# The second group norm's statistics taken inside the attention phase, by GpSimd

## The chip, the cores and the metric

One core of a Trainium2 chip (trn2) runs the whole kernel. The metric is the device time of one execution in microseconds, the median of several. TensorE (PE), VectorE (DVE), ScalarE (ACT), GpSimd (POOL) and SyncE (SP, which here only issues DMAs) run side by side and are ordered by semaphores alone.

## The reference, cut to what matters

The input `x` has 256 x 256 positions with 128 channels, f32. Two layers follow each other, both with a group norm (32 groups of 4 channels, statistics over all positions) at their head:

```python
def _gn(v, G=32, eps=1e-5):
    g = v.reshape(B_, H_, W_, G, C_ // G)
    m = jnp.mean(g, axis=(1, 2, 4), keepdims=True)
    s = jnp.var(g, axis=(1, 2, 4), keepdims=True)
    return ((g - m) / jnp.sqrt(s + eps)).reshape(v.shape)

x = x + attention(_gn(x))          # layer 0: rows of 256, 4 heads of 32
x = x + state_space(_gn(x))        # layer 1: conv, four scans, norm, product
```

The change touches the second `_gn` only, and of it only the two numbers for each group, mean and variance of the result of layer 0 (called `x1` here).

## The kernel before

The kernel is a sequence of phases with a barrier of all engines between them (`end_block`, L59 to L63): weights, `group_stats` "g0" on `x`, `norm_phase`, `attention_phase`, `group_stats` "g1" on `x1`, `conv_phase`, `scans_phase` (over 80% of the time), `output_phase`. All statements of a phase are unrolled, each engine has a program of its own, and an instruction waits on semaphores that count (`S["yev"]` at r + 1 means that row r has been added).

**Attention** (L285 to L544) runs over the 256 rows of the picture, r = 0 to 255. Each row is 256 positions x 128 channels, kept as [128 partitions, 2, 128]. The order on each engine is written out by hand, three rows deep: TensorE projects row r + 3, makes the scores of r + 2, turns the exponentials of r and mixes the values; ScalarE takes exponentials and moves results out of PSUM; VectorE adds the bias to the scores (L495), takes the row's maximum (L525), moves one head (L508), takes the reciprocal of the denominators (L504), gates (L529, L534), and adds the output product in PSUM to the row of `x` in the buffer `a_xt` (L516, semaphore `yev`). GpSimd has one operation a row: it spreads the eight reciprocals over 256 elements (L542, semaphore `spread`), and TensorE turns that tile (L418, `across`). SyncE stores eight rows of `a_xt` at a time to `x1` in DRAM (L357, a chunk; `a_xt` and `a_zt` hold four chunks), and then loads the next `zn_t` rows (L345) and `x` rows (L350) into the chunk that came free.

**The statistics** (`group_stats`, L66 to L141) read the tensor back from DRAM in four loads of 8 MB (L91) into two buffers, with `bn_stats` for each load and group on VectorE (L98, 128 in all), join them with `bn_aggr` for each group (L102, 32), and then work out the scale and the shift over the partitions: a product with a matrix of 1/128 (L130), small VectorE operations, a second product (L133), a root on ScalarE (L138), and for "g1" two columns with scale and shift of each channel (L122, L125).

**conv_phase** begins with one row loaded from `x1` (L608), turned and projected on TensorE, while VectorE clears the large buffer `c_xi` (L663) before the row may be put there.

Of the kernel before, what the change touches and what calls it, by code (L numbers as in the profile page):

```python
# [10 lines left out]
ALU = mybir.AluOpType  # L11
# [3 lines left out]
P = 128  # L15
# [36 lines left out]
def signals(sems, names):  # L52

    names = names.split()
    assert len(names) <= len(sems) and len(set(names)) == len(names)
    return dict(zip(names, sems))


def end_block(nc, sems):  # L59

    first = sems[0].num
    nc.vector.sem_clear(range(first, first + len(sems)))
    nc.all_engine_barrier()  # L63


def group_stats(nc, sems, name, x, eps, const, scale_row, shift_row, columns=None):  # L66

    CHUNK = BANK // PER_GROUP
    per_part = TOKENS // P
    chunks = per_part // CHUNK  # L70
    with ExitStack() as stack:
        m = Memory(nc, stack)
        xt = m.sb(f"{name}_x", [P, 2, CHUNK, C])
        st = m.sb(f"{name}_st", [P, GROUPS, chunks, 6])
        mv = m.sb(f"{name}_mv", [P, GROUPS, 2])
        avg = m.sb(f"{name}_avg", [P, GROUPS, 2])
        dev = m.sb(f"{name}_dev", [P, GROUPS])
        var = m.sb(f"{name}_var", [P, GROUPS])
        std = m.sb(f"{name}_std", [P, GROUPS])
        pick = m.sb(f"{name}_pick", [P, 2, GROUPS])  # L80
        total = m.ps(f"{name}_total", [P, 2, BANK])
        src = x.rearrange("(p j k) c -> j p k c", p=P, k=CHUNK)
        S = signals(sems, "load0 load1 stats aggr mean dev spread var std chain")

        with nc.Block() as block:
            @block.sync
            def _(e):
                for j in range(chunks):
                    if j >= 2:
                        e.wait_ge(S["stats"], j - 1)  # L90
                    e.dma_start(xt[:, j % 2], src[j]).then_inc(S[f"load{j % 2}"], DMA)  # L91

            @block.vector
            def _(e):
                for j in range(chunks):
                    e.wait_ge(S[f"load{j % 2}"], DMA * (j // 2 + 1))
                    for g in range(GROUPS):
                        last = e.bn_stats(st[:, g, j, :], xt[:, j % 2, :, g * PER_GROUP:(g + 1) * PER_GROUP])  # L98
                    last.then_inc(S["stats"], 1)
                e.wait_ge(S["stats"], chunks)  # L100
                for g in range(GROUPS):
                    last = e.bn_aggr(mv[:, g, :], st[:, g])  # L102
                last.then_inc(S["aggr"], 1)
                e.wait_ge(S["mean"], 1)
                e.tensor_copy(avg[:, :, :].rearrange("p g s -> p (g s)"), total[:, 0, 0:2 * GROUPS]).then_inc(S["chain"], 1)
                e.wait_ge(S["chain"], 1)
                e.tensor_tensor(dev[:, :], mv[:, :, 0], avg[:, :, 0], ALU.subtract).then_inc(S["chain"], 1)
                e.wait_ge(S["chain"], 2)
                e.tensor_tensor(dev[:, :], dev[:, :], dev[:, :], ALU.mult).then_inc(S["dev"], 1)
                e.wait_ge(S["spread"], 1)  # L110
                e.tensor_tensor(var[:, :], avg[:, :, 1], total[:, 1, 0:GROUPS], ALU.add).then_inc(S["chain"], 1)
                e.wait_ge(S["chain"], 3)
                e.tensor_scalar(var[:, :], var[:, :], eps, None, ALU.add).then_inc(S["var"], 1)
                e.wait_ge(S["std"], 1)
                e.reciprocal(scale_row[:, :], std[:, :]).then_inc(S["chain"], 1)
                e.wait_ge(S["chain"], 4)
                e.scalar_tensor_tensor(out=shift_row[:, :], in0=avg[:, :, 0], scalar=-1.0, in1=scale_row[:, :],
                                       op0=ALU.mult, op1=ALU.mult).then_inc(S["chain"], 1)
                if columns:
                    e.wait_ge(S["chain"], 5)  # L120
                    for i, row in enumerate((scale_row, shift_row)):
                        e.tensor_tensor(pick[:, i, :], row[:, :], const["group_of"][:, :], ALU.mult).then_inc(S["chain"], 1)  # L122
                    e.wait_ge(S["chain"], 7)
                    for i, column in enumerate(columns):
                        e.tensor_reduce(column[:, 0:1], pick[:, i, :], AX_X, ALU.add)  # L125

            @block.tensor
            def _(e):
                e.wait_ge(S["aggr"], 1)
                e.matmul(total[:, 0, 0:2 * GROUPS], const["mean"][:, :], mv[:, :, :].rearrange("p g s -> p (g s)"),  # L130
                         start=True, stop=True).then_inc(S["mean"], 1)
                e.wait_ge(S["dev"], 1)
                e.matmul(total[:, 1, 0:GROUPS], const["mean"][:, :], dev[:, :], start=True, stop=True).then_inc(S["spread"], 1)  # L133

            @block.scalar
            def _(e):
                e.wait_ge(S["var"], 1)
                e.activation(std[:, :], var[:, :], ACT.Sqrt).then_inc(S["std"], 1)  # L138
        end_block(nc, sems)
# [142 lines left out]
        end_block(nc, sems)  # L282


def attention_phase(nc, sems, x, zn_t, bias_d, x1, wts, const):  # L285

    N = SIDE
    CHUNK = zn_t.shape[2] // SIDE
# [3 lines left out]
    with ExitStack() as stack:  # L292
# [12 lines left out]
        spread = m.sb("a_spread", [P, 2, JB, C])  # L305
        factor = m.sb("a_factor", [P, 2, SIDE])
        gt = m.sb("a_gt", [P, 2, SIDE])
        scores = m.ps("a_scores", [P, HEADS, BANK])
        proj = m.ps("a_proj", [P, BANK])
        turn = m.ps("a_turn", [P, 2, BANK])  # L310
# [7 lines left out]
        with nc.Block() as block:  # L318
            @block.sync
            def _(e):  # L320
                for jb in range(JB):
                    e.dma_start(bias[:, jb], bsrc[jb]).then_inc(S["bias"], DMA)
                e.wait_ge(S["bias"], JB * DMA)
# [2 lines left out]
        at = lambda r: r % (SLOTS * CHUNK)  # L326
        head = lambda h: slice(h * HEAD_DIM, (h + 1) * HEAD_DIM)
        S = signals(sems, "loadz0 loadz1 loadz2 loadz3 loadx0 loadx1 loadx2 loadx3 store0 store1 store2 store3 "
                          "qk qkev vg gate vev score sev top exp turned tev_dve tev_act pv rden spread across factor gated ymm yev")

        def turned_out(e, r, h):

# [5 lines left out]
        with nc.Block() as block:  # L338
            @block.sync
            def _(e):  # L340
                def load(q):
                    slot, first = q % SLOTS, q % SLOTS * CHUNK
                    if q >= SLOTS:
                        e.wait_ge(S["vg"], (q - SLOTS + 1) * CHUNK)
                    e.dma_start(zt[:, first:first + CHUNK], zsrc[q]).then_inc(S[f"loadz{slot}"], DMA)  # L345
                    if q >= SLOTS:
                        e.wait_ge(S[f"store{slot}"], DMA * (q // SLOTS))
                    for part in range(2):
                        here, there = first + part * CHUNK // 2, q * CHUNK + part * CHUNK // 2
                        e.dma_start(xt[:, here:here + CHUNK // 2], xsrc[:, there:there + CHUNK // 2]).then_inc(S[f"loadx{slot}"], DMA)  # L350

                for q in range(SLOTS):
                    load(q)
                for q in range(N // CHUNK):
                    here, rows = q % SLOTS * CHUNK, slice(q * CHUNK, (q + 1) * CHUNK)
                    e.wait_ge(S["yev"], (q + 1) * CHUNK)
                    e.dma_start(xdst[:, rows], xt[:, here:here + CHUNK]).then_inc(S[f"store{q % SLOTS}"], DMA)  # L357
                    if q + SLOTS < N // CHUNK:
                        load(q + SLOTS)
                for slot in range(SLOTS):  # L360
                    e.wait_ge(S[f"store{slot}"], DMA * (N // CHUNK // SLOTS))
# [173 lines left out]

            @block.gpsimd
            def _(e):
                for r in range(N):
                    e.wait_ge(S["rden"], r + 1)
                    if r >= 2:  # L540
                        e.wait_ge(S["across"], r - 1)
                    e.tensor_copy(spread[:, r % 2].rearrange("p b (h d) -> p b h d", h=HEADS),  # L542
                                  rden[:, r % 2].unsqueeze(3).to_broadcast([P, JB, HEADS, HEAD_DIM])).then_inc(S["spread"], 1)
        end_block(nc, sems)  # L544


# [1194 lines left out]
def build(nc, x, dram, out, eye, mean, group_of, one_row):  # L1741
# [11 lines left out]
    with ExitStack() as stack:  # L1753
# [48 lines left out]

        group_stats(nc, sems, "g0", x, 1e-5, const, scale_row, shift_row)
        norm_phase(nc, sems, x, zn_t, bias_d, wts, const, scale_row, shift_row)
        attention_phase(nc, sems, x, zn_t, bias_d, x1, wts, const)
        group_stats(nc, sems, "g1", x1, 1e-5, const, scale_row, shift_row, (scale_col, shift_col))
        conv_phase(nc, sems, x1, xc_tok, xc_own, wts, const, scale_col, shift_col)
        own = [{"proj": wts["proj"][k % 2], "dt_w": wts["dt_w"][k], "a_neg": wts["a_neg"][k], "d_diag": d_diag}
               for k in range(DIRECTIONS)]
# [55 lines left out]
```

## Time and profile before

| | us |
|---|---|
| median of 3 runs (24476.09 to 24478.5) | 24477.81 |
| the profiled execution, its own time | 24484.89 |
| its span, first to last instruction | 24483.1 |
| attention's steady rows, a row | 6.7 |
| mean granted TensorE clock over the span | 0.989 |

Busy time over the whole span: PE 97%, DVE 96%, ACT 92%, POOL 85%. Times of instructions are counted in us from the start of the span; "mean ns" is that of one instruction of a group; a bracket behind a row gives the idle time of the engine ahead of it and what ended it.

### The profile page before, as it was taken

What the parts mean: (1) busy time and instruction counts of PE and PEld (TensorE: products, weight loads), DVE (VectorE), ACT (ScalarE), POOL (GpSimd) and SP (SyncE); (2) the same over time, 40 slices, a digit from 0 to 9 for tenths busy, and PEclk for the clock granted to TensorE, in tenths of its full rate; (3) what the DMA queues carried; (4) which work ended last, traced back from release to release, by engine and by line L of the source; (5) the groups of instructions that cost most, each with busy time, mean ns of one, the idle gap of its engine ahead of it and who ended that gap; (6) DMA issues with size and microseconds to landing.
All of it is one profiled execution on the core that took longest, in us unless ns stands there. A gap on an engine that the chain in (4) does not pass through costs nothing. (4 is left out here: it accounts for less than half of the span.)

```text
span 24483.1 us, 521206 instructions
## 1 busy us (share of the span) xinstructions
PE 23673.9 (97%) x197836; PEld 21232.5 (87%) x197836; DVE 23428.3 (96%) x23356; ACT 22643.4 (92%) x45591; POOL 20836.7 (85%) x6924
## 2 busy tenths in 40 slices
PE   4997989999999999999999999999999999999999
PEld 1776469999999999999999899999999999999987
DVE  6999889999999999999999999999999999999996
ACT  3997569999999999999999999999999999999986
POOL 5000039999999999999999999999999999999997
PEclk8998999999999999999999999999999999999999
DMA  5222555555555555555555566666666666666665
GB/s 185 58 58 94 176 183 184 187 182 188 184 187 186 179 188 189 189 187 190 189 187 190 187 195 195 194 197 193 197 196 190 194 197 192 198 193 195 196 198 189
DMA packets 3815251, 4429.66 MB, mean 181 GB/s; under 512 B 2085380, under 2 KB 3140520, under 8 KB 3532584
## 3 DMA queue, kind: packets, MB, share of 16 engines
q1 hardware_dynamic: 3812776, 4396.31, 55.4%
q8 instruction: 1597, 26.17, 0.5%
q14 instruction: 878, 7.19, 0.1%
HBM read 3782.68 MB, written 617.09 MB: 180 GB/s over the span
## 5 line engine op out<-in xcount | busy, mean ns | idle before, releaser
L1470 DVE TENSOR_TENSOR_SCAN s_h<-s_da,s_h,s_db 128x512 f32<-128x512 f32 x16256 | 19208.5, 1260 | 251.2 <-PE s_db L1371 250.5
L1488 POOL TENSOR_TENSOR s_prod<-s_h,s_cb 128x2048 f32<-128x2048 f32 x4096 | 18617.4, 4574 | 448.8 <-DVE s_h L1470 440.9
L1440 ACT ACTIVATE s_da<-s_delta,a_neg 128x512 f32<-128x512 f32 x16384 | 10895.5, 716 | 181.8 <-DVE s_h L1470 149.2
L1384 PE MATMUL s_py<-eye,s_prod 128*128 128x128 f32 x65536 | 8505.7, 273 | 18.2 <-POOL s_prod L1488 17.6
L1429 ACT ACTIVATE s_dxb<-s_dx,s_btok 128x256 f32<-128x256 f32 x18944 | 8411.7, 502 | 32.1 <-PEq L63 32.1
L1371 PE MATMUL s_db<-s_bdiag,s_dx 128*128 128x128 f32 x51200 | 8399.5, 275 | 0.0
L1384 PEld LDWEIGHTS s_py<-eye,s_prod 128*128 128x128 f32 x65536 | 7416.1, 141 | 27.6 <-POOL s_prod L1488 22.4
L1367 PE MATMUL s_db<-eye,s_dxb 128*128 128x128 f32 x39936 | 7178.5, 276 | 156.2 <-ACT s_dxb L1429 116.9
L1371 PEld LDWEIGHTS s_db<-s_bdiag,s_dx 128*128 128x128 f32 x51200 | 7012.3, 192 | 0.0
L1367 PEld LDWEIGHTS s_db<-eye,s_dxb 128*128 128x128 f32 x39936 | 4806.9, 141 | 1156.4 <-issue 626.4
L542 POOL COPY a_spread<-a_rden 128x256 f32<-128x256 f32 x256 | 103.1, 403 | 1646.0 <-DVE a_rden L504 1646.0
L459 ACT ACTIVATE a_sc<-a_sc,a_ntop 128x256 f32<-128x256 f32 x2048 | 1015.6, 501 | 0.0
L1100 POOL TENSOR_TENSOR s_dx<-s_delta,s_xc 128x1024 f32<-128x1024 f32 x384 | 914.2, 2381 | 12.9 <-DVE s_delta L1087 12.9
L850 POOL COPY c_xi<-c_xi 128x1032 f32<-128x1032 f32 x7 | 7.4, 1050 | 932.4 <-ACT c_xi L641 932.4
L1394 PE MATMUL s_py<-s_yb,eye 128*128 128x512 f32 x1536 | 786.2, 594 | 0.0
L842 DVE SCALAR_TENSOR_TENSOR c_acc<-c_xi,w_conv_w,c_acc 128x1024 f32<-128x1024 f32 x576 | 740.1, 1285 | 20.6
L495 DVE SCALAR_TENSOR_TENSOR a_sc<-a_scores,a_bias 128x512 f32<-128x512 f32 x1024 | 656.2, 682 | 72.2 <-PE a_scores L384 40.6
L1260 ACT COPY s_yt<-s_py 128x512 f32<-128x512 f32 x1024 | 540.4, 578 | 168.6 <-PE s_py L1384 168.5
L1065 ACT ACTIVATE s_dx<-s_pr 128x1024 f32<-128x1024 f32 x512 | 522.2, 1020 | 168.0 <-PE s_pr L1024 168.0
L1087 DVE SCALAR_TENSOR_TENSOR s_delta<-s_dx,s_pr 128x1024 f32<-128x1024 f32 x512 | 617.3, 1206 | 9.5 <-ACT s_dx L1068 5.7
L525 DVE TENSOR_REDUCE a_ntop<-a_sc 128x8 f32<-128x2048 f32 x256 | 585.2, 2286 | 8.8
L1024 PE MATMUL s_pr<-s_low,w_dt_w 9*128 9x512 f32 x2048 | 578.0, 641 | 0.4 <-DVE s_btok L1081 0.4
(139 smaller groups left out, 16397.8 us busy)
## 6 DMA issues: line engine op xcount, KB each, us to landing
s_cb<-c_rows SPq DMA_DIRECT2D x2048, 1024.0 KB, 5.5
s_bdiag<-b_diag SPq DMA_DIRECT2D x2048, 256.0 KB, 5.1
s_bdiag<-b_diag SPq DMA_DIRECT2D x1536, 192.0 KB, 6.7
y<-s_yt SPq DMA_DIRECT2D x1024, 256.0 KB, 2.7
s_xc<-xc_own SPq DMA_DIRECT2D x384, 512.0 KB, 9.3
s_yb<-y SPq DMA_DIRECT2D x768, 256.0 KB, 4.2
xc_tok<-c_ot SPq DMA_DIRECT2D x32, 2048.0 KB, 7.6
s_xt<-xc_tok SPq DMA_DIRECT2D x256, 256.0 KB, 5.3
```

The costliest lines, as they stand in the source:

```text
L459: last = e.activation(sc[:, r % 3, h, jb, :], sc[:, r % 3, h, jb, :], ACT.Exp, bias=ntop[:, r % 3, h, jb:jb + 1], accum_out=den[:, r % 2, ...
L495: e.scalar_tensor_tensor(out=sc[:, r % 3, h, :, :], in0=scores[:, h, :].rearrange("p (b k) -> p b k", b=JB), scalar=SCALE, in1=bias[:, :, ...
L842: last = e.scalar_tensor_tensor(out=into, in0=window, scalar=w, in1=into, op0=ALU.mult, op1=ALU.add)
L1100: e.tensor_tensor(e1(s), delta[:, s], xc[:, s], ALU.mult).then_inc(S["doubled"], 1)
L1367: e.transpose(db[:, i % NDB, half, j * P:(j + 1) * P], dxb[:, i % NDXB, j, half * P:(half + 1) * P], const["eye"][:, :])
L1371: last = e.matmul(db[:, i % NDB, half, j * P:(j + 1) * P], dx[:, g % 2, j, half * P:(half + 1) * P], columns, start=True, stop=True)
L1384: last = e.matmul(out, prod[:, i // TOGETHER % GROUPS_KEPT, i % TOGETHER, half, j * P:(j + 1) * P], const["eye"][:, :], start=first, stop= ...
L1394: last = e.matmul(py[:, bank, :], const["eye"][:, :], flat(yb[:, subs, :]), start=False, stop=False, skip_group_check=True)
L1429: last = e.activation(dxb[:, i % NDXB, j, :], dx[:, g % 2, j, :], ACT.Copy, scale=btok[:, g % 2, 0, j, n:n + 1])
L1440: last = e.activation(da[:, i % NDA, half, :], delta[:, g % 2, half, :], ACT.Exp, scale=wts[k]["a_neg"][:, half, n:n + 1])
L1470: last = e.tensor_tensor_scan(h[:, n, half, flow], da[:, i % NDA, half, flow], db[:, i % NDB, half, flow], first, ALU.mult, ALU.add)
L1488: e.tensor_tensor(prod[:, p % GROUPS_KEPT], h[:, states], columns.unsqueeze(2).to_broadcast([P, TOGETHER, HALVES, T]), ALU.mult).then_inc( ...
```

## The change

`group_stats` is split in two: the reading and `bn_stats` part stays for "g0" alone, and what follows it becomes `group_scales`, which is handed a function that fills `mv` (mean and mean of squares, or variance, for each partition and group). For "g1" the sums come out of the attention phase: a tile `sums` [128, 2, 2, 128] is cleared by GpSimd, and for each row, two rows after the row has been added, GpSimd squares the row into `a_square`, adds the row to `sums[:, 0]`, and adds the square to `sums[:, 1]`. SyncE waits for these before it reloads a chunk of `a_xt`. After attention VectorE reduces `sums` to groups and works out mean and variance of each partition.

```diff
@@ attention_phase, SyncE
                     e.dma_start(xdst[:, rows], xt[:, here:here + CHUNK]).then_inc(S[f"store{q % SLOTS}"], DMA)
                     if q + SLOTS < N // CHUNK:
+                        e.wait_ge(S["stats"], 2 * (q + 1) * CHUNK)
+                        e.wait_ge(S["square"], (q + 1) * CHUNK)
                         load(q + SLOTS)
@@ attention_phase, GpSimd
+                def statistics(r):
+                    e.wait_ge(S["yev"], r + 1)
+                    if r >= 2:
+                        e.wait_ge(S["stats"], 2 * (r - 1))
+                    e.tensor_tensor(square[:, r % 2], xt[:, at(r)], xt[:, at(r)], ALU.mult).then_inc(S["square"], 1)
+                    if r >= 1:
+                        e.wait_ge(S["stats"], 2 * r)
+                    e.tensor_tensor(sums[:, 0], sums[:, 0], xt[:, at(r)], ALU.add).then_inc(S["stats"], 1)
+                    e.wait_ge(S["square"], r + 1)
+                    e.tensor_tensor(sums[:, 1], sums[:, 1], square[:, r % 2], ALU.add).then_inc(S["stats"], 1)
+
+                e.memset(sums[:, :, :, :].rearrange("p s b c -> p (s b c)"), 0.0).then_inc(S["plain"], 1)
+                e.wait_ge(S["plain"], 1)
                 for r in range(N):
                     e.wait_ge(S["rden"], r + 1)
                     if r >= 2:
                         e.wait_ge(S["across"], r - 1)
                     e.tensor_copy(spread[:, r % 2].rearrange("p b (h d) -> p b h d", h=HEADS),
                                   rden[:, r % 2].unsqueeze(3).to_broadcast([P, JB, HEADS, HEAD_DIM])).then_inc(S["spread"], 1)
+                    if r >= 2:
+                        statistics(r - 2)
+                for r in range(N - 2, N):
+                    statistics(r)
@@ build
-        group_stats(nc, sems, "g1", x1, 1e-5, const, scale_row, shift_row, (scale_col, shift_col))
+            def from_sums(e, S, mv):
+                each = 1.0 / (SIDE * (SIDE // P) * PER_GROUP)
+                for s in range(2):
+                    e.tensor_reduce(mv[:, :, s], sums[:, s].rearrange("p b (g c) -> p g b c", c=PER_GROUP),
+                                    mybir.AxisListType.XY, ALU.add).then_inc(S["part"], 1)
+                e.wait_ge(S["part"], 2)
+                e.tensor_scalar(mv[:, :, :], mv[:, :, :], each, None, ALU.mult).then_inc(S["part"], 1)
+                e.wait_ge(S["part"], 3)
+                e.tensor_tensor(sums[:, 0, 0, 0:GROUPS], mv[:, :, 0], mv[:, :, 0], ALU.mult).then_inc(S["part"], 1)
+                e.wait_ge(S["part"], 4)
+                e.tensor_tensor(mv[:, :, 1], mv[:, :, 1], sums[:, 0, 0, 0:GROUPS], ALU.subtract).then_inc(S["aggr"], 1)
+
+            group_scales(nc, sems, "g1", from_sums, 1e-5, const, scale_row, shift_row, (scale_col, shift_col))
...
```

## Rows read from the trace of the kernel before

**Rows 1.** The page's first line: the span.

```profile
span 24483.1 us, 521206 instructions
```

**Rows 2.** Busy time of each engine over attention's rows, clock, DMA share.

```profile
600.00:2320.00 1720.00, 1711.12 (x16336) 1322.43 (x16336) 1663.67 (x2553) 1675.73 (x5628) 103.13 (x256) 1.00 0.20 57
```

**Rows 3.** Timeline of one row of attention: start, us, instruction, [idle before].

```profile
2232.22 0.40 POOL L542 COPY a_spread<-a_rden 128x256 f32<-128x256 f32 x1 [6.31 <-DVE a_rden L504]
...
2234.05 0.41 DVE L516 TENSOR_TENSOR a_xt<-a_mix,a_xt 128x256 f32<-128x256 f32 x1
...
2235.00 0.38 PE L418 MATMUL a_mix<-eye,a_spread 128*128 128x128 f32 x2
...
2238.94 0.40 POOL L542 COPY a_spread<-a_rden 128x256 f32<-128x256 f32 x1 [6.31 <-DVE a_rden L504]
```

**Rows 4.** Timeline from attention's last row to the joined statistics.

```profile
2322.79 0.42 DVE L516 TENSOR_TENSOR a_xt<-a_mix,a_xt 128x256 f32<-128x256 f32 x1 [0.80 <-PE a_mix L391]
2323.24 0.36 SPq L357 DMA_DIRECT2D x<-a_xt  x1
2329.48 60.75 SPq L91 DMA_DIRECT2D g_x<-x  x4
2329.48 1.28 ACT L138 ACT_TABLE_LOAD   x1 [9.65 <-PEq L63]
2351.48 19.10 DVE L98 BATCH_NORM_STATS2 g_st<-g_x 128x6 f32<-128x512 f32 x32 [28.26 <-DMA g_x<-x]
...
2433.14 4.04 DVE L102 BATCH_NORM_AGGREGATE g_mv<-g_st 128x2 f32<-128x24 f32 x32
2437.24 0.50 PEld L130 LDWEIGHTS g_total<-g_mv,mean 128*128 128x128 f32 x2 [114.68 <-DVE g_mv L102]
```

**Rows 5.** Costs of small VectorE operations, grouped by form.

```profile
L525 DVE TENSOR_REDUCE a_ntop<-a_sc 128x8 f32<-128x2048 f32 x256 | 585.2, 2286 | 8.8
...
L109 DVE TENSOR_TENSOR g_dev<-g_dev 128x32 f32<-128x32 f32 x2 | 0.4, 193 | 0.1
```

**Rows 6.** Timeline of the conv phase's first instructions on SyncE and VectorE.

```profile
2442.25 31.80 SPq L608 DMA_DIRECT2D c_xt<-x  x12
...
2445.99 14.68 DVE L663 MEMSET c_xi<- 128x17544 f32 x1 [4.70 <-issue]
```

**Rows 7.** Busy times and clock between attention and the conv phase.

```profile
2322.80:2466.00 143.20, 4.08 (x10) 2.46 (x10) 99.23 (x182) 2.72 (x5) 0.00 (x0) 0.50 0.59 246
```

**Rows 8.** GpSimd's operations of other phases, grouped by form.

```profile
L1488 POOL TENSOR_TENSOR s_prod<-s_h,s_cb 128x2048 f32<-128x2048 f32 x4096 | 18617.4, 4574 | 448.8 <-DVE s_h L1470 440.9 <-issue 2.8
L1100 POOL TENSOR_TENSOR s_dx<-s_delta,s_xc 128x1024 f32<-128x1024 f32 x384 | 914.2, 2381 | 12.9 <-DVE s_delta L1087 12.9
L1500 POOL TENSOR_SCALAR s_dxb<-s_dx,s_btok 128x256 f32<-128x256 f32 x1024 | 503.3, 491 | 14.9 <-POOLq L63 7.8 <-PE s_db L1371 7.1
...
L1650 POOL TENSOR_TENSOR o_yn<-o_yn,o_zs 128x512 f32<-128x512 f32 x128 | 167.3, 1312 | 172.9 <-ACT o_zs L1682 172.9
```

**Rows 9.** DMA issues in attention's rows: count, KB each, median us to landing.

```profile
a_zt<-zn_t SPq DMA_DIRECT2D x27, 1024.0 KB, 9.0
```

**Rows 10.** Durations (ns, min/median/max) of VectorE's L1626 in the output phase.

```profile
L1626 DVE TENSOR_TENSOR o_yn<-o_yn,o_zs x128: 656/693/2592, 23843.8 to 24474.4; 128x512 f32<-128x512 f32 x128
```

**Rows 11.** Durations (ns, min/median/max) of VectorE's L1609 in the output phase.

```profile
L1609 DVE TENSOR_TENSOR o_ot<-o_op,o_x x128: 676/691/692, 23849.6 to 24478.6; 128x512 f32<-128x512 f32 x128
```

**Rows 12.** Timeline of the output phase, VectorE alone.

```profile
23860.78 0.68 DVE L1609 TENSOR_TENSOR o_ot<-o_op,o_x 128x512 f32<-128x512 f32 x1
...
23867.30 2.56 DVE L1626 TENSOR_TENSOR o_yn<-o_yn,o_zs 128x512 f32<-128x512 f32 x1 [0.88 <-ACT o_zs L1682]
```

**Rows 13.** The same stretch, GpSimd alone.

```profile
23860.70 1.30 POOL L1650 TENSOR_TENSOR o_yn<-o_yn,o_zs 128x512 f32<-128x512 f32 x1 [4.84 <-ACT o_zs L1682]
...
23866.83 2.49 POOL L1650 TENSOR_TENSOR o_yn<-o_yn,o_zs 128x512 f32<-128x512 f32 x2
```

**Rows 14.** Durations of a VectorE operation with operands like L529, in the scans.

```profile
L1087 DVE SCALAR_TENSOR_TENSOR s_delta<-s_dx,s_pr x512: 1182/1199/1240, 3414.8 to 23732.7; 128x1024 f32<-128x1024 f32 x171
```

**Rows 15.** Busy times in a stretch of the scans.

```profile
20000.00:20500.00 500.00, 499.11 (x4237) 467.92 (x4236) 489.58 (x417) 483.39 (x922) 485.51 (x115) 1.00 0.62 193
```

More of the change, by code:

```diff
@@ L63, in end_block, with group_stats @@
     nc.all_engine_barrier()
-def group_stats(nc, sems, name, x, eps, const, scale_row, shift_row, columns=None):
+def group_stats(nc, sems, name, x, eps, const, scale_row, shift_row):
     CHUNK = BANK // PER_GROUP
@@ L74, in group_stats @@
         st = m.sb(f"{name}_st", [P, GROUPS, chunks, 6])
[L75 to L81, printed above, removed]
         src = x.rearrange("(p j k) c -> j p k c", p=P, k=CHUNK)
-        S = signals(sems, "load0 load1 stats aggr mean dev spread var std chain")
+        S = signals(sems, "load0 load1 stats")
         with nc.Block() as block:
@@ L99, in _, with joined, group_scales @@
                     last.then_inc(S["stats"], 1)
[L100 to L103, printed above, removed]
+        end_block(nc, sems)
+        def joined(e, S, mv):
+            for g in range(GROUPS):
+                last = e.bn_aggr(mv[:, g, :], st[:, g])
+            last.then_inc(S["aggr"], 1)
+        group_scales(nc, sems, name, joined, eps, const, scale_row, shift_row)
+def group_scales(nc, sems, name, reduce, eps, const, scale_row, shift_row, columns=None):
+    with ExitStack() as stack:
+        m = Memory(nc, stack)
+        mv = m.sb(f"{name}_mv", [P, GROUPS, 2])
+        avg = m.sb(f"{name}_avg", [P, GROUPS, 2])
+        dev = m.sb(f"{name}_dev", [P, GROUPS])
+        var = m.sb(f"{name}_var", [P, GROUPS])
+        std = m.sb(f"{name}_std", [P, GROUPS])
+        pick = m.sb(f"{name}_pick", [P, 2, GROUPS])
+        total = m.ps(f"{name}_total", [P, 2, BANK])
+        S = signals(sems, "part aggr mean dev spread var std chain")
+        with nc.Block() as block:
+            @block.vector
+            def _(e):
+                reduce(e, S, mv)
                 e.wait_ge(S["mean"], 1)
@@ L282, in norm_phase, with attention_phase @@
         end_block(nc, sems)
-def attention_phase(nc, sems, x, zn_t, bias_d, x1, wts, const):
+def attention_phase(nc, sems, x, zn_t, bias_d, x1, wts, const, sums):
     N = SIDE
@@ L307, in attention_phase @@
         gt = m.sb("a_gt", [P, 2, SIDE])
+        square = m.sb("a_square", [P, 2, JB, C])
         scores = m.ps("a_scores", [P, HEADS, BANK])
@@ L328, in attention_phase @@
         S = signals(sems, "loadz0 loadz1 loadz2 loadz3 loadx0 loadx1 loadx2 loadx3 store0 store1 store2 store3 "
-                          "qk qkev vg gate vev score sev top exp turned tev_dve tev_act pv rden spread across factor gated ymm yev")
+                          "qk qkev vg gate vev score sev top exp turned tev_dve tev_act pv rden spread across factor gated ymm yev square plain stats")
         def turned_out(e, r, h):
@@ L1804, in build @@
         norm_phase(nc, sems, x, zn_t, bias_d, wts, const, scale_row, shift_row)
-        attention_phase(nc, sems, x, zn_t, bias_d, x1, wts, const)
-        group_stats(nc, sems, "g1", x1, 1e-5, const, scale_row, shift_row, (scale_col, shift_col))
+        with ExitStack() as inner:
+            sums = Memory(nc, inner).sb("g1_sums", [P, 2, SIDE // P, C])
+            attention_phase(nc, sems, x, zn_t, bias_d, x1, wts, const, sums)
+            def from_sums(e, S, mv):
[10 more added lines that the diff above has]
+            group_scales(nc, sems, "g1", from_sums, 1e-5, const, scale_row, shift_row, (scale_col, shift_col))
         conv_phase(nc, sems, x1, xc_tok, xc_own, wts, const, scale_col, shift_col)
```

## The prediction

> **What bounds the kernel now.** I read the page's head first: the span is 24483.1 us [rows 1], the profiled execution as a whole took 24484.89, and the runs have a median of 24477.81, 7.1 below it. I sum against the profiled execution and take the difference off the median. Then the table of busy times by stretch. In attention's rows (600 to 2320) TensorE is busy 1711 of 1720 us, ScalarE 1676, VectorE 1664, GpSimd 103, at full clock (1.00, so 2.4 GHz) [rows 2]. The reader should see that three engines have almost no slack there and GpSimd has nearly all of it. The timeline of one row gives the period: L542 starts at 2232.22 and again at 2238.94, so 6.7 us, of which GpSimd stands idle 6.31 [rows 3]. Last the timeline between attention and the conv phase: the last row is added by 2323.21, the phase opens for "g1" at 2329.48, its first load lets VectorE start at 2351.48, the joined statistics are there at 2437.18 (2433.14 + 4.04), and TensorE's product starts at 2437.24 after 114.68 us of nothing [rows 4]. All other engines wait in that stretch, so its length is paid in full.
>
> **What is removed.** From 2329.48 to 2437.18, four loads with `bn_stats` behind them and 32 `bn_aggr`: 107.7 us. None of it lies beside other work [rows 4].
>
> **What takes its place at that spot.** VectorE has two reductions of 256 elements and three small operations. L525 reduces 2048 elements in 2286 ns, 1.1 ns an element; 256 of them and a fixed part of the order of L109's 193 ns give about 0.4 us each, 0.8 for two. A small operation like L109 takes 0.193, about 0.23 with the chained start, so 0.7 for three [rows 5]. Together 1.5 us; bounds 1.0 (all five at 0.193) and 5.4 (both reductions at L525's full 2.29, three small ones). The first VectorE instruction of a phase may come late: the conv phase's first one (L663) starts at 2445.99, while SyncE already issued at 2442.25, so 3.7 us late, for no reason that the trace names [rows 6]. I take 1 us, between nothing and 3.7. ScalarE's table load for the root (1.28 us from 2329.48 [rows 4]) was hidden under the statistics. Now the load ends at 2330.8 as before, and the root stands behind the statistics (2331.0 at the earliest), two products and four small VectorE operations: 0. The clock changes nothing: it is 0.50 (1.2 GHz) on the mean of 2322.80 to 2466, TensorE having worked 4 us in all that time [rows 7]. So it fell as soon as attention's products ended, in the wait for the last store, and conv starts at half clock either way. Sum here: -107.7 + 1.5 + 1.0 = -105.2 us.
>
> **What is added in attention.** Three GpSimd operations with two SBUF inputs, 256 elements each, a row. The trace has such operations at 2048 elements (L1488, 4574 ns) and 1024 (L1100, 2381 ns), hence 2.14 ns an element and 0.19 us fixed. For 512 this gives 1.28 us, and L1650 shows 1.31. For 256 it gives 0.74 us. Bounds: 0.49 (L1500, as many elements with one input) and 1.31 (L1650, twice as many) [rows 8]. A row's statistics take 2.2 us (1.5 to 3.9), and with the spread 2.6 (1.9 to 4.3), in a period of 6.7.
>
> *Who waits for it.* `statistics(r - 2)` stands behind the spread of row r in GpSimd's queue. Its `yev` came one row earlier (L516 at 2234.05 belongs to the row before), so it starts at once, at 2232.62, and ends by 2234.9, at the worst bound 2236.6. The next spread is asked for at 2238.9, and a spread is done 2.4 us before L418, the product that reads it, starts (2232.62 to 2235.00) [rows 3]. So nothing queued behind is late, and the cost is 0 while the three take less than 6.3 us together. The memset of `sums` runs while TensorE projects the first rows, 0.
>
> *SyncE.* The reload of a chunk now also waits for statistics two rows behind `yev`, 13.4 + 3 us. Row 8q + 32, the first of that chunk, is projected at iteration 8q + 29 and asked for at about 8q + 10: 19 rows, 127 us, against a landing of 9.0 us [rows 9]. The next store in the queue is due eight rows after the last, 54 us. Cost 0.
>
> *The end.* After the last add at 2323.21 one row's statistics remain, 2.2 us, to 2325.4, under the last store, whose landing opens the next phase at 2329.48 [rows 4]. Cost 0, for 3.9 us too.
>
> **Does GpSimd slow the engines that have no slack?** This decides the sign. Two cases are in the output phase. L1626 has both inputs in SBUF, takes 693 ns at the median and up to 2592 [rows 10]. Its 2.56 us from 23867.30 [rows 12] end just behind the pair of GpSimd operations at 23866.83 that took 2.49 [rows 13]: VectorE was held until GpSimd let go. L1609 has one input in PSUM and one in SBUF, and never took over 692 ns in 128 times [rows 11], among them 0.68 at 23860.78 [rows 12], inside a GpSimd two-input operation from 23860.70 to 23862.00 [rows 13]. In attention no VectorE operation has two inputs in SBUF: L495, L516, L529 and L534 have one operand in PSUM, L508 reads PSUM, L504 and L525 have one input. L516 is L1609's kind exactly, and L1087, of L529's kind, stays between 1182 and 1240 ns all through the scans [rows 14], where GpSimd is busy 485 of 500 us, and TensorE still 499 and ScalarE 483 at full clock [rows 15]. I take 0. Upper bound: L1609's spread, 692 over 676 or 2.4%, on VectorE's 6.5 us a row is 0.16 us, some 40 us over 256 rows, if VectorE's 0.2 us of slack a row hid none of it.
>
> The Trainium skill (SBUF — State Buffer, Who interferes with whom) speaks against work handed from VectorE to GpSimd: the two share one pair of ports, held for a whole instruction, against VectorE instructions with two SBUF inputs or in a two-port mode; one with at most one SBUF input outside those modes is left alone. The trace agrees on both sides with L1626 and L1609. By that rule attention keeps its period; read as holding every VectorE operation, it would give the first rival below.
>
> **The sum.** 24484.89 - 105.2 = 24379.7 for a profiled execution; 24477.81 - 105.2 = 24372.6 for the median. The gain is 0.43%.
>
> **Rivals.**
> 1. *GpSimd holds VectorE in attention.* If each of the three operations held back a VectorE operation for its whole 0.74 us, a row grows by up to 2.2 us, 256 rows by 567, and the time is 24372.6 + 567 = 24940, slower. It decides from 0.41 us a row (105.2 / 256). For it: L1626's 2592 ns. Against: L1609, L1087. Chance 0.04.
> 2. *GpSimd becomes the bound of attention.* From (6.7 - 0.4) / 3 = 2.1 us an operation. At 2.6, the longest that a neighbour shows [rows 10], a row takes 0.4 + 7.8 = 8.2, 1.5 us more, so 384 more: 24757, slower. For it: three operations chained by semaphores, never seen so here. Against: 2048 elements take 4.57. Chance 0.02.
> 3. *A small drag in every row.* 0.22 to 0.6 us a row (3 to 9% of VectorE) gives 56 to 154 us back, within 0.2% of before, about 24478. Against: the 2.4% above. Chance 0.04. A drag under 0.2 us leaves 24380 to 24423, still faster: chance 0.08.
> 4. *Part of the gain returns in conv's entry*, by late first instructions: up to 3.7 us twice, 24380, inside the range.
>
> **How the numbers follow.** The forecast with rival 4 has 0.82. Its own range is from 24362 to 24385: 3 us below if the replacement costs nothing, some more for where the clock steps fall, and above it 3.9 for the replacement's bound with 7 for late instructions. The small drag's bound takes the top to 24412. I give 24360 to 24412. About 0.2% (49 us) is what a measurement of this kernel tells from no change. Faster 0.82 + 0.08 = 0.90, within 0.2% 0.04, slower 0.06.
>
> **What would show it.** After: attention's period still 6.7 us, TensorE still at 99% there; three GpSimd operations of about 0.74 us behind each spread, idle of some 4 us left before the next; L516 at 0.41 us as before; product L130's counterpart some 2.5 us after the phase opens, and no load before it; all later phases moved as a block. It is wrong if VectorE operations in attention show a longer maximum with GpSimd beside them, if `a_spread` is what TensorE waits for, or if the conv phase takes longer by what "g1" lost.

## The result and the profile after

The changed kernel takes 24372.74 us (median of 5, 24371.61 to 24375.43), the kernel before beside it 24477.98. The ratio is 0.9957 with a 95% interval of 0.9945 to 0.9968: 105.2 us less, where 105.2 were forecast. The interval allows 78 to 135 us, so the agreement to a tenth says little; the profiles below say more. The profiled execution took 24371.61 with a span of 24369.8. The profiled execution of before was 7 us above its median, so the difference of the two spans, 113.3 us, is not the effect alone; where its parts lie is told below.

GpSimd's groups of instructions in the changed kernel, by form; they answer to [rows 8]:

```profile
L564 POOL TENSOR_TENSOR g_sums<-g_sums,a_xt 128x256 f32<-128x256 f32 x256 | 188.3, 735 | 0.0
L566 POOL TENSOR_TENSOR g_sums<-g_sums,a_square 128x256 f32<-128x256 f32 x256 | 187.1, 731 | 0.0
...
L561 POOL TENSOR_TENSOR a_square<-a_xt 128x256 f32<-128x256 f32 x256 | 157.1, 614 | 1.6 <-DVE a_xt L535 1.6
L574 POOL COPY a_spread<-a_rden 128x256 f32<-128x256 f32 x256 | 101.7, 397 | 1137.3 <-DVE a_rden L523 1137.3
```

The timeline of one attention row after, all engines, as [rows 3]:

```profile
2230.13 0.40 POOL L574 COPY a_spread<-a_rden 128x256 f32<-128x256 f32 x1 [4.36 <-DVE a_rden L523]
...
2230.49 0.61 POOL L561 TENSOR_TENSOR a_square<-a_xt 128x256 f32<-128x256 f32 x1
...
2231.06 0.73 POOL L564 TENSOR_TENSOR g_sums<-g_sums,a_xt 128x256 f32<-128x256 f32 x1
...
2231.75 0.73 POOL L566 TENSOR_TENSOR g_sums<-g_sums,a_square 128x256 f32<-128x256 f32 x1
...
2232.90 0.38 PE L437 MATMUL a_mix<-eye,a_spread 128*128 128x128 f32 x2
...
2236.84 0.40 POOL L574 COPY a_spread<-a_rden 128x256 f32<-128x256 f32 x1 [4.36 <-DVE a_rden L523]
```

The period is 6.71 us, the same as before, and GpSimd's idle time in it went from 6.31 to 4.36. The spread is still ready 2.4 us before L437 (L418 before) reads it. Busy times of attention's rows after, against [rows 2]:

```profile
600.00:2320.00 1720.00, 1710.17 (x16341) 1321.55 (x16333) 1664.30 (x2554) 1674.79 (x5626) 599.56 (x1021) 1.00 0.19 56
```

TensorE 1710 for 1711, VectorE 1664 for 1664, ScalarE 1675 for 1676, GpSimd 600 for 103. Last the timeline from the last row to the conv phase, against [rows 4] and [rows 6]:

```profile
2320.70 0.42 DVE L535 TENSOR_TENSOR a_xt<-a_mix,a_xt 128x256 f32<-128x256 f32 x1 [0.80 <-PE a_mix L410]
2321.15 0.36 SPq L374 DMA_DIRECT2D x<-a_xt  x1
...
2322.45 0.72 POOL L566 TENSOR_TENSOR g_sums<-g_sums,a_square 128x256 f32<-128x256 f32 x1
2327.38 1.28 ACT L154 ACT_TABLE_LOAD   x1 [9.63 <-PEq L63]
2327.43 0.75 DVE L1848 TENSOR_REDUCE g_mv<-g_sums 128x32 f32<-128x256 f32 x2 [6.30 <-PEq L63]
...
2328.66 0.19 DVE L1855 TENSOR_TENSOR g_mv<-g_mv,g_sums 128x32 f32<-128x32 f32 x1
2328.90 0.50 PEld L146 LDWEIGHTS g_total<-g_mv,mean 128*128 128x128 f32 x2 [8.43 <-DVE g_mv L1855]
...
2333.92 37.20 SPq L644 DMA_DIRECT2D c_xt<-x  x15
...
2337.65 14.68 DVE L699 MEMSET c_xi<- 128x17544 f32 x1 [4.70 <-issue]
```

From the phase's opening (2327.38) to joined statistics (2328.85) it is 1.47 us, for 107.7 before: 106.2 us gained at that spot. From the last store to the opening it is 6.2 us as before, so the last rows' statistics (done at 2323.17) are under it. From the joined statistics to the conv phase's first load it is 5.07 us in both.

The change costs something at a second spot. Where `group_stats` was split, "g0" now has a barrier between its reading and its joining. In the kernel before, `bn_aggr` follows the last `bn_stats` at once (the row before it ends at 131.36):

```profile
131.39 4.04 DVE L102 BATCH_NORM_AGGREGATE g_mv<-g_st 128x2 f32<-128x24 f32 x32
```

In the changed kernel VectorE stands idle for 1.03 us between the two:

```profile
131.85 4.04 DVE L97 BATCH_NORM_AGGREGATE g_mv<-g_st 128x2 f32<-128x24 f32 x32 [1.03 <-PEq L63]
```

The 1.03 us are the same in the profile of every kernel below that was made from the changed one. So the net step is 106.2 - 1.0 = 105.2 us.

The other 7.1 us (113.3 - 106.2) between the two profiled executions are scatter between executions. The first projection of attention starts 2.2 us earlier in spite of the barrier (587.18 for 589.35), the conv phase is 1.9 shorter, scans and output together 3.1. In the changed kernel's second measurement (below) that projection starts at 589.39, and in the other kernels of this document between 584.51 and 592.50.

### The profile page after: what moved, and what is told of

Read it like the earlier page. It is cut to its first block and busy times, and to the rows that moved or that the text cites. A ratio compares the mean times of both kernels' runs of the same rounds, so it can differ in the third digit from the quotient of the medians.

```text
span 24369.8 us, 522122 instructions
## 1 busy us (share of the span) xinstructions
PE 23668.9 (97%) x197836; PEld 21230.2 (87%) x197836; DVE 23347.7 (96%) x23201; ACT 22643.5 (93%) x45591; POOL 21329.9 (88%) x7693
## 5 line engine op out<-in xcount | busy, mean ns | idle before, releaser
L1465 ACT ACTIVATE s_dxb<-s_dx,s_btok 128x256 f32<-128x256 f32 x18944 | 8418.7, 503 | 32.7 <-PEq L63 32.7
L514 DVE SCALAR_TENSOR_TENSOR a_sc<-a_scores,a_bias 128x512 f32<-128x512 f32 x1024 | 656.0, 682 | 70.9 <-PE a_scores L403 40.2
L544 DVE TENSOR_REDUCE a_ntop<-a_sc 128x8 f32<-128x2048 f32 x256 | 585.2, 2286 | 8.8
```

The costliest lines, as they stand in the source:

```text
L514: e.scalar_tensor_tensor(out=sc[:, r % 3, h, :, :], in0=scores[:, h, :].rearrange("p (b k) -> p b k", b=JB), scalar=SCALE, in1=bias[:, :, ...
L1465: last = e.activation(dxb[:, i % NDXB, j, :], dx[:, g % 2, j, :], ACT.Copy, scale=btok[:, g % 2, 0, j, n:n + 1])
```

## The experiments

**Attention's work without the gain.** The changed attention, but the second norm reads `x1` back as before.

```diff
             attention_phase(nc, sems, x, zn_t, bias_d, x1, wts, const, sums)
-            group_scales(nc, sems, "g1", from_sums, 1e-5, const, scale_row, shift_row, (scale_col, shift_col))
+        group_stats_read(nc, sems, "g1", x1, 1e-5, const, scale_row, shift_row, (scale_col, shift_col))
...
```

> The row's statistics are taken by GpSimd in attention, but their sums are not used: the second group norm reads x1 back with bn_stats as in the kernel before. Theory (GpSimd's work is free): attention's period stays 6.71 us and the time is that of before, 24478, within 3 us. Rival 'small drag': anything from 24490 (0.05 us a row) to 24530 (0.2 us a row). Rival 'GpSimd holds VectorE': about 25040.

Measured: 24484.07 against 24483.22 for the kernel before beside it, ratio 1.0 (0.9991 to 1.0009). 0.85 us for 256 rows is no drag that the measurement tells, and this kernel too has the barrier in "g0", which alone makes 1.0 us.

**The gain without the work.** GpSimd sets the sums once (to 0 and 512) and takes no statistics, so the second norm works with a made-up mean and variance. SyncE's two waits go as well.

```diff
...
-                    if r >= 2:
-                        statistics(r - 2)
-                for r in range(N - 2, N):
-                    statistics(r)
...
```

> Left out: the statistics themselves; GpSimd sets the sums to constants once (sum 0, sum of squares 512), so the second norm works with a made-up mean and variance. Neither attention's work nor the reading of x1 is there. Theory: the time is that of the changed kernel, 24373, within 3 us, since what it leaves out costs nothing there. Rival 'small drag': lower than 24373 by 256 times the drag, 13 us for 0.05 us a row.

Measured: 24376.15, or 107.1 less than before on the same chip. The changed kernel had 105.2 less in its first measurement and 105.8 in its second (below). So the medians leave the work some 2 us at most, no more than two measurements differ by. The profiles are sharper: from attention's first projection to its last store it is 1733.9 us before, 1734.0 changed, 1733.7 here, and 1732.2 in the kernel above, which does all the work.

**The same work on VectorE.** The three operations moved behind the row's add.

```diff
                         e.tensor_tensor(xt[:, at(q)]..., mix[:, 0:SIDE], xt[:, at(q)]..., ALU.add).then_inc(S["yev"], 1)
...
+                        e.tensor_tensor(square[:, q % 2], xt[:, at(q)], xt[:, at(q)], ALU.mult).then_inc(S["square"], 1)
+                        e.tensor_tensor(sums[:, 0], sums[:, 0], xt[:, at(q)], ALU.add).then_inc(S["stats"], 1)
...
+                        e.tensor_tensor(sums[:, 1], sums[:, 1], square[:, q % 2], ALU.add).then_inc(S["stats"], 1)
```

> The same three operations a row, on VectorE right behind the row's add instead of on GpSimd two rows later. Theory (the gain rests on GpSimd having nothing to do): VectorE is busy 6.5 of 6.7 us a row, three operations of 0.33 to 0.41 us start to start make 7.5 to 7.7, so 0.8 to 1.0 us a row more, 205 to 256 us: 24578 to 24629, slower than before. Rival 'the loop has room on VectorE too, TensorE alone sets it': 24373 to 24400.

Measured: 24633.94, ratio 1.0062 (1.0048 to 1.0076), 150.7 slower than before and 257.8 over the kernel that takes no statistics, just above the 205 to 256 that I expected. VectorE's timeline gives the row:

```profile
2261.52 0.19 DVE L523 RECIPROCAL a_rden<-a_den 128x8 f32<-128x8 f32 x1
...
2263.90 0.43 DVE L542 TENSOR_TENSOR a_square<-a_xt 128x256 f32<-128x256 f32 x1
2264.24 0.42 DVE L543 TENSOR_TENSOR g_sums<-g_sums,a_xt 128x256 f32<-128x256 f32 x1
2264.58 0.42 DVE L545 TENSOR_TENSOR g_sums<-g_sums,a_square 128x256 f32<-128x256 f32 x1
...
2269.22 0.19 DVE L523 RECIPROCAL a_rden<-a_den 128x8 f32<-128x8 f32 x1
```

7.70 us for 6.71, 0.99 x 256 = 253. The additions are shorter here than on GpSimd (0.42 for 0.73), and still it is the wrong engine: 0.41 us a row (105.2 / 256) was all that there was to give away.

**More work for GpSimd**, nine and fifteen operations a row in place of three.

```diff
...
+                    for i in range(6):      # 12 in the second kernel
+                        if 6 * r + i >= 2:
+                            e.wait_ge(S["idle"], 6 * r + i - 1)
+                        e.tensor_tensor(idle[:, (6 * r + i) % 2], bias[:, :, 0, 0:C], bias[:, :, 1, 0:C], ALU.add).then_inc(S["idle"], 1)
```

> GpSimd does six further additions of 256 elements with two SBUF inputs for each row, into a tile nobody reads: nine such operations a row in all. From the changed kernel's rows (spread 0.36 start to start, square 0.57, others 0.69) GpSimd needs 0.36 + 0.57 + 8 x 0.69 = 6.45 of the 6.71 us. Theory: it fits, VectorE is never held, the time is 24373 to 24385, and GpSimd is over 93% busy in attention. Rival 'small drag proportional to GpSimd's work': three times the drag of the changed kernel, seen as up to 120 us more. Rival 'holds VectorE': over 25000.

> GpSimd does twelve further additions a row (fifteen two-input operations in all). Theory (GpSimd is free until its own row is longer than 6.71 us): 0.36 + 0.57 + 14 x 0.695 + 0.3 of waiting for the next reciprocal, 10.7 to 11.0 us a row, so 4.0 to 4.3 us x 256 = 1020 to 1100 us over the changed kernel: 25395 to 25475. Rival (the queue is buffered in some other way and the loop runs on for longer): less than 900 us over it.

Nine operations: 24381.43, 101.8 less than before beside it. The busy times of its attention rows:

```profile
600.00:2320.00 1720.00, 1708.51 (x16328) 1321.19 (x16328) 1664.29 (x2553) 1672.54 (x5618) 1646.02 (x2542) 1.00 0.19 56
```

GpSimd is busy 96% and the others as before; attention's length is 1733.75 us. What is lost lies behind it: GpSimd's queue of the last rows runs on to 2332.60, while the last store was issued at 2318.26, and the next phase opens at 2333.62. That is 15.4 us behind the last store in place of 6.2, so 9.1 more. The median shows only 5.3 of it beside the 107.1 of the kernel without statistics on the same chip. In this execution attention began at 584.51, earlier than in any other kernel here; why was not followed up.

Fifteen operations: 25355.78, 979.8 over the changed kernel beside it, less than the 1020 that I expected at least. GpSimd's timeline has a row of 10.5 us with no wait in it, where I had added 0.3, and TensorE's has the wait that was missing everywhere else (1.3 to 3.7 us in the rows looked at, 2.3 in the mean of 191):

```profile
3007.28 0.95 POOL L579 COPY a_spread<-a_rden 128x256 f32<-128x256 f32 x1
...
3017.78 0.96 POOL L579 COPY a_spread<-a_rden 128x256 f32<-128x256 f32 x1
```

```profile
3008.29 0.69 PE L438 MATMUL a_mix<-eye,a_spread 128*128 128x128 f32 x2 [3.68 <-POOL a_spread L579]
```

(10.50 - 6.71) x 256 = 970. Nine operations fit into the period and fifteen do not, and the loss is what GpSimd's own row is longer than TensorE's period, as the forecast has it. Where between the two the loss begins was not measured.

**Is it the PSUM operand that keeps VectorE free?** Four kernels with one more VectorE addition of 256 elements a row. Between the first and second bias addition, beside GpSimd's statistics: with two SBUF inputs, and with one in PSUM. With two SBUF inputs where GpSimd is idle: behind the row's maximum, and at the first place in the kernel before. The cut shows the first place.

```diff
                         biased(r + 2, 0)
+                        e.tensor_tensor(idle[:, 0]..., bias[:, 1, 0, :], bias[:, 0, 0, :], ALU.add)       # two in SBUF
+                        e.tensor_tensor(idle[:, 0]..., scores[:, 1, 0:SIDE], bias[:, 0, 0, :], ALU.add)   # one in PSUM
```

> The changed kernel with one more VectorE operation a row: an addition of 256 elements with both inputs in SBUF, into a tile nobody reads, put between the first and the second bias addition of a row, where GpSimd's statistics are under way (from 0.6 to 2.6 us behind the row's reciprocal). By its own length it costs 0.33 us start to start of which some 0.1 to 0.2 lie in VectorE's slack: 35 to 60 us. Theory (two SBUF inputs are held off by a GpSimd operation, and across operations that follow each other at once, as in the output phase): it also waits until GpSimd's last addition is done, up to 1.1 us more a row, so 150 to 350 us over the changed kernel. Rival (the hold of 2.56 us in the output phase had another cause): as the next two kernels, 35 to 60 us.

> The same addition at the same place, but its first input is 256 elements of the scores in PSUM and its second is in SBUF, the kind of attention's own VectorE operations. Theory: not held, 35 to 70 us over the changed kernel, and the operation's duration has a narrow spread around 0.41 us. Rival 'GpSimd holds any VectorE operation that reads SBUF': 150 to 350 us as with two SBUF inputs.

> The same addition with two SBUF inputs, put right behind the row's maximum, where GpSimd has nothing to do in the changed kernel. Theory: not held, 35 to 60 us over the changed kernel. Rival (what costs is the operation and not its neighbour): as much as at the first place.

> The same addition with two SBUF inputs at the first place, in the kernel before, where GpSimd only makes the spread. Theory: 35 to 60 us over the kernel before. Rival (the place is bad whatever GpSimd does): 150 to 350 us over the kernel before.

| kernel | median, us | against | difference |
|---|---|---|---|
| two in SBUF, beside GpSimd | 24539.58 | changed, 24375.7 | +163.9 |
| one in PSUM, beside GpSimd | 24406.02 | changed, 24375.7 | +30.3 |
| two in SBUF, GpSimd idle | 24412.66 | changed, 24375.7 | +37.0 |
| two in SBUF, kernel before | 24516.99 | before, 24480.97 | +36.0 |

(24375.7 is 0.9957 of the 24480.97 of the kernel before beside them; the changed kernel itself was not run beside them.) All came out as expected but the second, which is 5 us under its 35 to 70. The durations of the added instruction in the first kernel (ns, min/median/max):

```profile
L531 DVE TENSOR_TENSOR a_idle<-a_bias x256: 414/933/948, 600.0 to 2471.3; 128x256 f32<-128x256 f32 x128
```

and in the second, with the operand in PSUM:

```profile
L531 DVE TENSOR_TENSOR a_idle<-a_scores,a_bias x256: 412/413/416, 596.1 to 2334.8; 128x256 f32<-128x256 f32 x128
```

One moment of the first kernel, VectorE:

```profile
2103.80 0.94 DVE L531 TENSOR_TENSOR a_idle<-a_bias 128x256 f32<-128x256 f32 x1
2104.66 0.68 DVE L515 SCALAR_TENSOR_TENSOR a_sc<-a_scores,a_bias 128x512 f32<-128x512 f32 x1
```

and GpSimd:

```profile
2103.73 0.73 POOL L566 TENSOR_TENSOR g_sums<-g_sums,a_xt 128x256 f32<-128x256 f32 x1
2104.42 0.91 POOL L568 TENSOR_TENSOR g_sums<-g_sums,a_square 128x256 f32<-128x256 f32 x1
```

VectorE's addition starts 0.07 us behind L566 and takes 0.94 us for 0.41; L568 behind it is stretched to 0.91 for 0.73. 0.52 us x 256 = 133, and the first two kernels differ by 133.6. The place, the operation's length and GpSimd's load are the same in both; the operand alone decides. It is shown so for the form of L514, L535, L548 and L553 (one input in PSUM, one in SBUF).

For L523, L527 and L544 (a single input) the changed kernel shows little, since the statistics (2230.49 to 2232.48 in the row above) are over before L544 (2233.60) and L523 (2236.59) start, and L527 (2229.99, 0.64 us) meets them for 0.14 us. The kernel with nine operations settles it: GpSimd is busy 96% of the time there, and the row's maximum, the longest of the three, keeps its length in all 256 rows, 2285/2286/2287 in the kernel before:

```profile
L545 DVE TENSOR_REDUCE a_ntop<-a_sc x256: 2286/2286/2287, 593.9 to 2304.5; 128x8 f32<-128x2048 f32 x128
```

The reciprocal has 191/192/195 there for 191/191/194. Only the copy L527 has a longer maximum than in the kernel before (636/639/641). It has it without statistics beside it too, so they are not the cause. First the changed kernel, then the one without statistics:

```profile
L527 DVE COPY a_pt<-a_turn x256: 636/639/693, 606.0 to 2315.2; 128x512 f32<-128x512 f32 x128
L525 DVE COPY a_pt<-a_turn x256: 639/639/693, 609.7 to 2318.6; 128x512 f32<-128x512 f32 x128
```

The Trainium skill (SBUF — State Buffer, Who interferes with whom) has as its rule that a VectorE instruction with two SBUF inputs contends with a GpSimd instruction that reads SBUF, and that one with at most one SBUF input, outside the two-port modes, does not. All four kernels agree with it.

**The changed kernel again, and what is next in the chain.** With the reading gone, the clearing of `c_xi` is the longest piece between attention and conv's loop.

```diff
-                e.wait_ge(S["zero"], 1)
+                e.wait_ge(S["zero"], 3)
...
-                e.memset(xi[:, :, :, :].rearrange("p a r w -> p (a r w)"), 0.0).then_inc(S["zero"], 1)
+                e.memset(xi[:, :, 0, :], 0.0).then_inc(S["zero"], 1)
+                for side in (0, WIDE - 1):
+                    e.memset(xi[:, :, 1:TURN + 2, side:side + 1], 0.0).then_inc(S["zero"], 1)
```

> The changed kernel itself once more, beside the two others of this call on one chip. Every theory: 0.9957 of the kernel before, the difference between 103 and 108 us.

> The changed kernel, and in the conv phase's first block VectorE clears only the first row and the two outer columns of c_xi instead of all 17544 elements a partition (14.68 us); the rest is written before it is read. Theory (with the second reading gone, this clearing is the longest piece of the chain between attention and the conv loop: ScalarE's copy waits 15.13 us for it): 11 to 14 us less than the changed kernel, about 24360. Rival (the first loads of the conv loop come no earlier, or the clearing's end is not what the chain waits for): within 2 us of the changed kernel.

Measured: the changed kernel 24375.94 against 24481.75 (0.9957, 0.9943 to 0.9971), 105.8 less; with the edges alone 24364.35 (0.9952, 0.9939 to 0.9964), 11.6 less again and the fastest of all. Its timeline:

```profile
2336.83 23.06 SPq L644 DMA_DIRECT2D c_xt<-x  x15
2337.01 0.49 DVE L699 MEMSET c_xi<- 128x516 f32 x1 [1.15 <-PEq L63]
...
2341.64 0.37 ACT L677 COPY c_xi<-c_xp 128x256 f32<-128x256 f32 x1 [1.37 <-PE c_xp L669]
...
2355.41 0.75 DVE L877 TENSOR_SCALAR c_acc<-c_xi,w_conv_w 128x1024 f32<-128x1024 f32 x1 [16.06 <-ACT c_xi L677]
```

Conv's first filter operation comes 18.6 us after the phase's first load, for 32.7 in the changed kernel (2333.92 to 2366.64). That is 14.1 us less, where the medians show 11.6; the rest was not followed up.

## Why the prediction was right, step by step

- *The removed stretch*, 107.7 us with nothing beside it: right. No opening, store or table load took its place. The clock had indeed fallen in both: it is 0.50 over 2322.80 to 2360 after, as over 2322.80 to 2466 before.
- *The replacement*, 1.5 us: measured 1.42 (2327.43 to 2328.85).
- *The first VectorE instruction late by 1 us*: wrong in size. It started 0.05 us after ScalarE's. The step at this spot is then -106.2 and not -105.2.
- *The barrier that the split puts into "g0"*: missing in the prediction, which has no term for it. It costs 1.0 us (1.03 idle before L97, 0.03 in the kernel before). So the sum is right because two errors of 1 us cancel, and that is luck. The medians of two measurements, -105.2 and -105.8, are too coarse to tell such terms apart.
- *GpSimd's operations*, 0.74 us each: the two additions have 0.735 and 0.731, the square 0.614. Spread and statistics take 2.35 us of a row (6.71 - 4.36), for 2.6 predicted: each operation starts before the one ahead has its full recorded length behind it (0.57 us behind the square, 0.69 behind the first addition).
- *Who waits for GpSimd*: nobody in attention's loop. The cover is 4.36 us a row; six more operations fit into it and twelve do not.
- *SyncE*: the reload was predicted some 16 us behind the store. SyncE waited 136.6 and 36.7 us for GpSimd over 27 chunks, 6.4 us a chunk: `yev` of a row falls into the next row's turn already, so the statistics follow it by one row and not by two. Nothing hung on it.
- *GpSimd holds VectorE* (rival 1): not here, and for the reason given. One VectorE operation with both inputs in SBUF beside the statistics would have cost 134 us of contention, more than the whole gain. The prediction's sign of being wrong, a longer maximum of a VectorE operation, did show in L527 (693 for 641 ns), but as much without the statistics.
- *Small drag* (rival 3): attention's length moved by 0.1 us, and with nine operations a row it did not grow either (1733.75 us). Executions differ by up to 1.8 us in it, so a drag of more than some 0.01 us a row would show. *GpSimd as the bound* (rival 2): only with fifteen operations.
- *Conv's entry* (rival 4): unchanged, 3.73 us from the first load to the recorded start of the memset, for 3.74. The first filter operation comes 32.7 us behind that load for 34.1 before. That is no effect of the change either: in the other kernels with the same conv phase it is 32.4 to 33.6, and 33.7 in the kernel before with an added VectorE operation.

## What to carry to other kernels

A second reading of a result can be folded into the phase that makes it, if one engine has idle time there: what counts is that engine's idle time in a row (here 4.4 us left over), not that it is slower for the operation. Before handing work to GpSimd, list for each VectorE operation beside it where its inputs lie. Here those with one in PSUM, or only one at all, were left alone; one with two in SBUF paid 0.52 us each time, and in the output phase up to 1.9 us (2.56 for 0.69). When a phase is split, count the barrier that comes with it (1.0 us here). Then look at the chain again: the next piece here was a clearing of 14.7 us, small beside the 107.7 that are gone, and cutting it down gave 11.6 more.

## What the runs showed of the hardware

- The loser of the contention here got its turn between two GpSimd instructions that followed each other (0.94 us for 0.41), and the next GpSimd instruction waited in turn (0.91 for 0.73). In the output phase a VectorE operation lasted over two of them (2.56 us, [rows 12] and [rows 13]). I had expected that here too, up to 1.1 us a row more, and it was 0.52. What makes the difference was not tried.
- GpSimd's square of a row with itself took 0.61 us, its additions of two different tiles 0.73.
- The memset of 17544 elements starts 3.7 us late by its record and takes 14.68; the one of 516, at the same place, starts 0.18 us after SyncE's load and takes 0.49. 3.73 + 14.68 us are 1.05 ns an element and 0.49 us are 0.95, so the long one may well have begun at once and been recorded late. That is argued and was not tested.
- With fifteen operations a row TensorE waits for the spread in every row (440.1 us in 191 waits, 3.7 at most), and its mean granted clock over 1000 to 3000 fell to 0.85, for 1.00 in attention otherwise. L429, right behind the wait of 3.68 us, took 1.93 us for 1.07.
